# New tick tables for preparation and finishing, routing that ends one iteration later, rows of x that come one iteration earlier, and a fifth sum buffer

## The chip, the cores and the metric

One core of a Trainium2 chip runs the kernel. The metric is the device time of one launch in microseconds. TensorE (PE), VectorE (DVE), ScalarE (ACT), GpSimd (POOL) and SyncE (SP) each run their own instruction stream strictly in program order and meet only at semaphores. One profiled execution and three timed ones are at hand.

## The reference

For 16 batches of 128 rows of width 512, with 2048 context rows per batch:

```python
x = x + xattn(layernorm(x), ctx, ctx)   # 16 query heads of 32, ONE shared key head and value head
x = x + attn(layernorm(x))              # gated delta rule, 4 heads of 128, chunks of 64, needs inv(I - A0)
x = x + ffn(layernorm(x))               # top-1 routing to 16 experts, 128 rows each, relu(x w1) w2

# routing inside ffn
gate = softmax(xr @ Wg); idx = argmax(gate)
loc  = cumsum(onehot)[row, idx] - 1      # place of the row in its expert, over all earlier rows
valid = loc < C
dispatched[idx, min(loc, C)] = xr
```

All is float32. The count in `loc` runs over all 2048 rows, so the routing of one batch needs the counts of the batch before.

## The kernel before

The program has two blocks. `attention` handles the 16 batches; `experts` then runs the 16 experts from the rows that were scattered to DRAM. Only `attention` is touched.

`attention` is a software pipeline written by hand. The outer loop is `for i in range(-1, B + 1)`. Iteration `i` works on three batches at once: it does the softmax attention of batch `i`, prepares batch `i + 1` (norm of x, transposes of the context, keys, values, queries), and finishes batch `i - 1` (normalising the attention output, output projection, second norm, delta rule with six doubling levels, third norm, gate and routing). An iteration is cut into 128 ticks. Each engine's stream is generated by the same double loop over `i` and tick `t`, and a step is emitted at the tick that a table names. So the tables (`NORM`, `XN`, `XNT`, `QPROJ`, `TILE_AT`, `KV_AT`, `VT_AT`, `LOAD_AT`, `POST`, `LEVEL_AT`, `MAX_AT`) fix nothing but the order of each stream. A tick has no length of its own.

The steady work of batch `i`: at every even tick a score matmul (`score`, line 370) and its exponential on ACT (line 553). For each of four head groups 16 matmuls and DVE maxima of the next group (`largest`, lines 357 and 708), then the turn of the maxima (`turn_max`, line 362), whose row ACT copies (line 559) and SP sends. The probabilities times values in quads (`weigh`, line 382), two quads in one tick at ticks 1 and 17 of every group of 32. GpSimd adds up the probabilities over the 16 key blocks (`add_weights`, line 917) into one of four buffers `psum[g]`.

The seam between two batches matters for what follows. At tick 118 PE computes the gate logits (`lg`, line 508), DVE and ACT form the one-hot row (`oh`, lines 818 to 830), PE counts (`loc`, line 513, tick 123), DVE computes the target row in 14 small instructions (`row`, lines 834 to 860, tick 125), and GpSimd scatters. In the next iteration DVE normalises rows of x for the coming batch (lines 722 to 727, ticks 1 and 5), PE sums numerators and denominators (`sums`, line 396, tick 9), DVE takes four reciprocals (line 764, ticks 9 to 12) and multiplies (`att`, line 767, tick 13), and PE starts the output projection (`x1`, line 336 with `wo`, ticks 15 to 18). `sums` writes the same PSUM bank, `P_BANK`, that the routing read, and every later finishing step uses it too. The first addition into `psum[0]` of a batch waits for `sums` of the batch before (line 912). `TensorE` may issue the maxima matmul number n only when DVE has reduced number n - 2 (line 347).

Of the kernel before, what the change touches and what calls it, by code (L numbers as in the profile page):

```python
# [24 lines left out]
C_IDENT, C_UPPER, C_PAIR, C_ONES, C_DUMP, C_LEVEL = range(6)  # L25
# [24 lines left out]
PV_AT = [17, 17, 33, 33]  # L50
# [51 lines left out]
def attention(nc, T, w1_first, w1_in):  # L102
    with ExitStack() as ctx:
# [6 lines left out]
        def named(name, names):  # L110
# [30 lines left out]
        oS, psum = ([sb(f"{n}{g}", [P, 512]) for g in range(HG)] for n in ("oS", "psum"))  # L141
# [51 lines left out]
        post_pe = named("post_pe", "x1 xn2T V rkT I X1 Vn oT2 x2 xn3T lg loc")  # L193
        post_act = named("post_act", "ss0 ss1 ss2 ss3 xn2T rk0 rk1 rk2 rk3 V rkT X1 Vn oT2 xn3T eg")
        post_dve = named("post_dve", "x1 st2 mv2 xn2 XT1a MT IT x2 st3 mv3 xn3 lg0 lmax emax cand best oh "
                         "ohloc before loc valid locc row0 row d0 d1 sidx gate token token1")
        post_pool = named("post_pool", "xb ve2 rs2 x12 rm rn MT0 XT0 XT1 ve3 rs3")
# [3 lines left out]
        def level(b, lv, part=0):  # L201
# [5 lines left out]
        T_USES = [use for _, use in sorted(  # L207
            [(XNT, ("x", 0))] + [(t, ("t", k)) for k, t in enumerate(TILE_AT)]
            + [(t, ("v", c)) for c, t in enumerate(VT_AT)])]

        def turn_bank(b, use):
            return [T_BANK, *B_BANK, PV_BANK][T_USES.index(use) % 4] if b == 0 else T_BANK

        def turn_read(b, use):

            n = T_USES.index(use) - (4 if b == 0 else 1)
            if n < 0:
                return v_act.at(b - 1, 1) if b else None
            kind, i = T_USES[n]
            if kind == "x":  # L220
                return xnT_act.at(b)
            return cxT_act.at(b, i) if kind == "t" else v_act.at(b, i)
# [29 lines left out]
        def _(e):  # L252
# [30 lines left out]
            def send_queries(b):  # L283

                for part, src, ready in ((0, qh, q_act), (1, qh, q_act), (2, qs, q_pool)):
                    e.wait_ge(*ready.at(b))
                    for h in range(4):
                        e.dma_start(
                            qT[b % 2][part * HD:(part + 1) * HD, :].bitcast(F32).rearrange(
                                "d (g h t) -> d g h t", g=HG, h=4)[:, :, h, :],  # L290
                            src[h * HD:(h + 1) * HD, :].bitcast(F32).rearrange("d (g t) -> d g t", g=HG)).then_inc(
                            q_in.sem, 16)

            for i in range(-1, B + 1):
                for t in range(TICKS):
                    if t == XNT + 2 and i + 2 < B:
                        load_x(i + 2)
                    if t == QSEND and i + 1 < B:
                        send_queries(i + 1)
                    for b, g in groups_at(i, t, MAX_TURN):  # L300
                        send_max(b, g)
                    if t in LOAD_AT:
# [3 lines left out]
                    if t == 0 and i >= 1:  # L306
                        if i > 1:
                            e.wait_ge(*post_pe.at(i - 2, "Vn"))
# [3 lines left out]
                    if t == POST["store"] and i >= 1:  # L312
                        e.wait_ge(*post_dve.at(i - 1, "x2"))
                        e.dma_start(T["out"][i - 1], x2).then_inc(x2_out.sem, 16)
# [11 lines left out]
        def _(e):  # L326
# [59 lines left out]
            def sums(b):  # L386
# [3 lines left out]
                if b:  # L390
                    e.wait_ge(*post_dve.at(b - 1, "before"))
                if b + 1 < B:
                    e.wait_ge(*kvs_dve.at(b + 1, 3))
                for out, lhs, src in ((KV_BANK, cst[:, C_ONES, 0:HD], psum), (P_BANK, cst[:, C_STACK, 0:HD], oS)):
# [4 lines left out]
            def prepare(b, t):  # L399
# [6 lines left out]
                if t == QPROJ:  # L406
                    if b == 0:
                        e.wait_ge(*wq_in.at(0))
                    e.wait_ge(*kvs_dve.at(b, 0))
                    e.wait_ge(*xnT_act.at(b))  # L410
                if QPROJ <= t < QPROJ + HG:
                    cols = slice((t - QPROJ) * P, (t - QPROJ + 1) * P)
                    for c in range(DC):
                        ins = e.matmul(KV_BANK[:, cols], wq[:, c, cols], xnT[:, c, :], start=c == 0, stop=c == DC - 1)
                    if t == QPROJ + HG - 1:
# [10 lines left out]
                if t in KV_AT:  # L426
                    c = KV_AT.index(t)
                    e.wait_ge(*cxT_act.at(b, 4 * c + 3))
                    if c:
                        e.wait_ge(*kvs_dve.at(b, c - 1))  # L430
                    elif b:
                        e.wait_ge(*(o_dve.at(b - 2, "recip3") if b > 1 else kvs_dve.at(0, 3)))
                    if c == 1:
                        e.wait_ge(*q_dve.at(b))
# [10 lines left out]
            def finish(b, t):  # L445
# [3 lines left out]
                if t == POST["x1"]:  # L449
                    e.wait_ge(*o_dve.at(b, "att"))  # L450
                if POST["x1"] <= t < POST["x1"] + DC:
                    ins = project(P_BANK, turned, wo, t - POST["x1"])
                    if t == POST["x1"] + DC - 1:
# [4 lines left out]
                if t == POST["V"]:  # L458
                    e.wait_ge(*post_act.at(b, "xn2T"))
                if POST["V"] <= t < POST["V"] + DC:  # L460
                    ins = project(P_BANK, turned, ww, t - POST["V"])
                    if t == POST["V"] + DC - 1:
# [27 lines left out]
                if t == POST["Vn"]:  # L490
                    e.wait_ge(*xt_dve.at(*level(b, LEVELS - 1, 3)))
                    per_head(P_BANK, lambda h: cut(XT, h), lambda h: cut(V, h)).then_inc(post_pe.sem, 1)
                if t == POST["oT2"]:
                    e.wait_ge(*post_act.at(b, "Vn"))
                    per_head(P_BANK, lambda h: cut(Vn, h), lambda h: cut(IT, h)).then_inc(post_pe.sem, 1)
                if t == POST["x2"]:
                    e.wait_ge(*post_act.at(b, "oT2"))
                if POST["x2"] <= t < POST["x2"] + DC:
                    ins = project(P_BANK, turned, wr, t - POST["x2"])
                    if t == POST["x2"] + DC - 1:  # L500
                        ins.then_inc(post_pe.sem, 1)
                if t == POST["xn3T"]:
                    e.wait_ge(*post_dve.at(b, "xn3"))
                    transposes(P_BANK, lambda h: cut(xn3, h)).then_inc(post_pe.sem, 1)
                if t == POST["lg"]:
                    e.wait_ge(*post_act.at(b, "xn3T"))
# [3 lines left out]
                    ins.then_inc(post_pe.sem, 1)  # L510
                if t == POST["loc"]:
                    e.wait_ge(*post_dve.at(b, "oh"))
                    e.matmul(P_BANK[:, 0:E], cst[:, C_UPPER, :], oh[:], start=True, stop=False)
                    e.matmul(P_BANK[:, 0:E], cst[:, C_ONES, :], before[:], start=False, stop=True).then_inc(
                        post_pe.sem, 1)
# [710 lines left out]
```

## Time and profile before

| | us |
|---|---|
| median of 3 timed runs (2423.36 to 2426.57) | 2425.18 |
| profiled execution, its own time | 2427.98 |
| span in the profile | 2426.1 |

The span is the time from the first to the last instruction of the profiled execution. The rest of its own time, 1.9 us, lies around it. In the profile the main part of the program is the run of iterations 0 to 15, whose first exponentials start at 70.8, 162.9, 287.0 and from there about every 117.8 us up to 1817.7. The experts begin at 2001.5.

### The profile page before, as it was taken

The numbers are of one execution on the slowest core, as the hardware profiler recorded it, in microseconds if no ns is written. First come the engines' busy times: TensorE is split into PE (matmuls) and PEld (weight loads), VectorE is DVE, ScalarE is ACT, GpSimd is POOL, SyncE is SP. The second block draws the span as 40 slices with busy tenths as digits, with TensorE's granted clock in tenths as the row PEclk, the third lists the DMA queues.
The fourth block names the chain that finished last, engine by engine and source line by source line (L and its number), as shares of the span: only waits on it lengthen the run. The fifth ranks groups of instructions, "written<-read, shape, count | busy, mean of one in ns | idle before, by whom it ended". The sixth has DMA issues, their size and how long they took to land. (4 is left out here: it accounts for less than half of the span.)

```text
span 2426.1 us, 35019 instructions
## 1 busy us (share of the span) xinstructions
PE 2189.4 (90%) x12608; PEld 1429.9 (59%) x12608; DVE 1371.0 (57%) x2311; ACT 1193.3 (49%) x2237; POOL 1638.2 (68%) x1323
## 2 busy tenths in 40 slices
PE   5889898989998989898989898989898769999999
PEld 3435555546464646464646464645554448999998
DVE  2665757566667566666666666666665433333333
ACT  3555554646464646464645455555554313333333
POOL 0676878677777777777777777777777714655655
PEclk9889998999899989998999899989998889999999
DMA  4532120202020202121211111121120009999995
GB/s 160 188 113 66 40 82 24 83 23 83 23 83 23 83 26 80 40 66 40 66 47 58 51 59 63 43 66 42 59 79 9 18 14 375 350 363 346 362 363 189
DMA packets 108157, 263.75 MB, mean 109 GB/s; under 512 B 9849, under 2 KB 35065, under 8 KB 99792
## 3 DMA queue, kind: packets, MB, share of 16 engines
q1 hardware_dynamic: 98448, 235.32, 27.7%
q10 hardware_dynamic: 5952, 14.29, 1.6%
q0 software_dynamic: 3584, 11.90, 1.2%
q8 instruction: 101, 1.65, 0.3%
q14 instruction: 72, 0.59, 0.1%
HBM read 223.74 MB, written 25.72 MB: 103 GB/s over the span
## 5 line engine op out<-in xcount | busy, mean ns | idle before, releaser
L917 POOL TENSOR_TENSOR psum<-psum,p 128x512 f32<-128x512 f32 x896 | 1162.9, 1298 | 291.7 <-ACT p L553 197.7
L708 DVE TENSOR_REDUCE mpart<-bank 128x1 f32<-128x512 f32 x1024 | 675.0, 682 | 403.5 <-PE bank L357 396.1
L553 ACT ACTIVATE p<-bank 128x512 f32<-128x512 f32 x1024 | 596.8, 600 | 553.5 <-PE bank L370 543.6
L357 PE MATMUL bank<-kT,qT 96*128 96x512 f32 x1024 | 484.1, 480 | 62.6 <-DVE mpart L708 32.5
L370 PE MATMUL bank<-qT,kT 97*128 97x512 f32 x1024 | 502.4, 492 | 4.7 <-ACT p L553 4.0
L357 PEld LDWEIGHTS bank<-kT,qT 96*128 96x128 f32 x1024 | 199.6, 196 | 211.5 <-DVE mpart L708 104.6
L370 PEld LDWEIGHTS bank<-qT,kT 97*128 97x128 f32 x1024 | 201.7, 197 | 142.6 <-issue 113.6
L382 PE MATMUL bank<-p,v 128*32 128x512 f32 x2048 | 271.4, 651 | 0.0
L1159 POOL TENSOR_TENSOR w2l<-w,w2h 128x1024 fp32r<-128x1024 f32 x64 | 203.2, 3177 | 75.1 <-PE ebank L1074 54.4
L332 PE MATMUL bank<-cst,w_first 128*128 128x128 f32 x1024 | 164.1, 287 | 21.7 <-DMA w_first<-in_ctx 18.0
L332 PEld LDWEIGHTS bank<-cst,w_first 128*128 128x128 f32 x1024 | 134.3, 149 | 64.9 <-issue 29.4
L917 POOL TENSOR_TENSOR psum<-p 128x512 f32<-128x512 f32 x64 | 81.8, 1278 | 122.5 <-ACT p L553 101.6
L582 ACT COPY w_first<-bank 128x512 f32<-128x512 f32 x256 | 149.3, 586 | 15.0 <-PE bank L332 14.9
L1102 ACT ACTIVATE hh<-ebank 128x512 fp32r<-128x512 f32 x64 | 38.3, 599 | 225.3 <-PE ebank L1058 225.3
L1096 ACT CAST w2h<-w 128x2048 fp32r<-128x2048 f32 x64 | 121.5, 1898 | 44.1 <-DMA w<-in_w 44.1
L382 PEld LDWEIGHTS bank<-p,v 128*32 128x32 f32 x2048 | 56.7, 116 | 141.7 <-issue 107.3
L437 PE MATMUL bank<-w_first,wkv 128*64 128x512 f32 x512 | 125.7, 612 | 10.0 <-ACT w_first L582 9.8
L336 PE MATMUL bank<-wo,turned 128*128 128x512 f32 x128 | 90.3, 799 | 38.8 <-DVE turned L767 38.8
L1058 PE MATMUL ebank<-dT,w_first 128*128 128x128 f32 x1024 | 120.9, 279 | 0.9 <-DVE dT L1117 0.9
L1058 PEld LDWEIGHTS ebank<-dT,w_first 128*128 128x128 f32 x1024 | 120.0, 195 | 2.4 <-issue 1.2
L1123 DVE TENSOR_TENSOR w2l<-w,w2h 128x1024 fp32r<-128x1024 f32 x64 | 79.1, 1236 | 71.9 <-PE ebank L1074 48.0
L1128 DVE SCALAR_TENSOR_TENSOR hl<-ebank,hh 128x512 fp32r<-128x512 f32 x64 | 44.2, 691 | 133.4 <-ACT hh L1102 133.4
(159 smaller groups left out, 3137.8 us busy)
## 6 DMA issues: line engine op xcount, KB each, us to landing
w<-in_w SPq DMA_DIRECT2D x48, 2048.0 KB, 20.1
w_first<-in_ctx SPq DMA_DIRECT2D x64, 1024.0 KB, 4.9
w_first<-in_w SPq DMA_DIRECT2D x16, 2048.0 KB, 11.6
dispatched<-route ACTq DMA_DIRECT2D x17, 513.0 KB, 4.4
dis<-dispatched SPq DMA_DIRECT2D x16, 513.0 KB, 3.5
qT<-qh SPq DMA_DIRECT2D x128, 64.0 KB, 2.0
xin<-in_x SPq DMA_DIRECT2D x16, 256.0 KB, 2.6
qT<-qs SPq DMA_DIRECT2D x64, 64.0 KB, 2.0
```

What stands on the lines that cost most here:

```text
L332: ins = e.transpose(out[0:m, j * P:(j + 1) * P], src(j), ident)
L357: e.matmul(a[:], qT[b % 2][0:3 * HD, (4 * g + h) * P:(4 * g + h + 1) * P], kT[b % 2][0:3 * HD, c * 512:(c + 1) * 512], start=True, stop=Tr ...
L370: e.matmul(B_BANK[u % 2][:], kT[b % 2][0:3 * HD + 1, k * P:(k + 1) * P], qT[b % 2][0:3 * HD + 1, g * 512:(g + 1) * 512], start=True, stop= ...
L382: ins = e.matmul(PV_BANK[HD * j:HD * (j + 1), :], v1[b % 2][:, k + j, :], p[(UNITS * b + u + j) % NP][:], start=k == 0, stop=k == KB - 4)
L437: ins = e.matmul(KV_BANK[rows, :], wkv[:, j, :], cxT[c % 2][:, j, :], start=j < 2, stop=j >= 2)
L553: e.activation(p[n % NP][:], B_BANK[u % 2][:], ACT.Exp).then_inc(p_act.sem, 1)
L582: e.copy(cxT[c % 2][:, :, kk * P:(kk + 1) * P], turn_bank(b, ("t", k))[:].rearrange("p (c t) -> p c t", c=DC)).then_inc(cxT_act.sem, 1)
L708: e.tensor_reduce(mpart[g % 2][:, n:n + 1], A_BANK[(17 * g + n) % 2][:], AX.X, ALU.max).then_inc(max_dve.sem, 1)
L917: e.tensor_tensor(acc[:], first[:], p[(UNITS * b + u) % NP][:], ALU.add).then_inc(psum_pool.sem, 1)
L1058: ins = e.matmul(H_BANK[g][:, f * P:(f + 1) * P], w1[q][:, c, (4 * g + f) * P:(4 * g + f + 1) * P], dT[q][:, c, :], start=c == 0, stop=c = ...
L1096: e.copy(w2h[g][:], w2[q][:, 4 * g:4 * g + 4, :]).then_inc(w2h_act.sem, 1)
L1159: e.tensor_tensor(w2l[g % 2][:, 2:4, :], w2[q][:, 4 * g + 2:4 * g + 4, :], w2h[g][:, 2:4, :].bitcast(F32), ALU.subtract).then_inc(w2l_pool ...
```

## The change

The tables get new numbers. Rows of x are loaded, normalised and transposed an iteration earlier than the rest of a batch's preparation: `NORM`, `XN` and `XNT` become negative, that is ticks 81, 82 and 89 of the iteration before. The finishing of a batch now reaches past tick 127: `oh` is at 129, `loc` at 133, `row` at 135, which are ticks 1, 5 and 7 of the second next iteration. `sums` goes from tick 9 to 10, the reciprocals from 9 to 12 to 9, 12, 13, 14, `att` from 13 to 15, `x1` from 15 to 18 to 18 to 21. The context tiles, no longer four ticks apart, stand one to eight apart. All four loops run over `range(-2, B + 2)`, the last one only up to `TAIL`. The semaphores of finishing are split into an early and a late set. `KV_BANK` and the transpose banks get their waits from a computed order of uses. There are five buffers for the sums of probabilities instead of four, used in turn, and the wait for `sums` moves from the first group of a batch to the second. The constant `C_DUMP` moves into a free column of `C_STACK`. `send_queries` gets a wait for the last score matmul of two batches before. No arithmetic is changed.

```diff
-NORM, XN, XNT, QPROJ, QSEND = 1, 5, 10, 27, 38
-TILE_AT = [8 + 4 * k for k in range(KB)]
-KV_AT = [TILE_AT[4 * c + 3] + 3 for c in range(4)]
-VT_AT = [KV_AT[2 * m + 1] + 7 for m in range(2)]
-LOAD_AT = [t + 6 for t in TILE_AT[3::4]]
-POST = dict(xb=2, sums=9, recip=[9, 10, 11, 12], att=13, x1=15, x1_add=18, norm2=19, xn2=22, ss=23, x12=24, rn=24,
-            xn2T=25, rk=27, V=28, V_copy=31, rkT=34, I=38, XT1=40, X1=44, Vn=98, oT2=101, x2=104, x2_add=107,
-            store=108, norm3=108, xn3=111, xn3T=115, lg=118, eg=119, oh=120, loc=123, row=125)
-LEVEL_AT = [[47 + 9 * n, 50 + 9 * n, 53 + 9 * n] for n in range(LEVELS)]
-MAX_AT, MAX_TURN = [15 * n // 8 - 39 for n in range(KB)], -8
+NORM, XN, XNT, QPROJ, QSEND = -47, -46, -39, [22, 26, 27, 29], 32
+TILE_AT = [9, 13, 14, 16, 19, 23, 27, 32, 35, 40, 44, 51, 54, 58, 61, 69]
+KV_AT = [20, 36, 59, 74]
+VT_AT = [42, 79]
+LOAD_AT = [20, 46, 55, 71]
+POST = dict(xb=4, sums=10, recip=[9, 12, 13, 14], att=15, x1=[18, 19, 20, 21], x1_add=23, norm2=22, xn2=25, ss=29,
+            x12=32, rn=34, xn2T=34, rk=37, V=[37, 38, 39, 40], V_copy=40, rkT=42, I=45, XT1=44, X1=49, Vn=100,
+            oT2=102, x2=[106, 107, 108, 109], x2_add=110, store=116, norm3=114, xn3=119, xn3T=122, lg=127, eg=127,
+            oh=129, loc=133, row=135)
+LEVEL_AT = [[50, 53, 56], [59, 62, 65], [68, 71, 74], [77, 80, 83], [85, 88, 90], [94, 97, 102]]
+TAIL = POST["row"] + 1 - TICKS
+MAX_AT = [-40, -38, -36, -34, -32, -29, -28, -26, -24, -23, -21, -19, -17, -15, -13, -11]
+MAX_TURN, PV_AT = -9, [17, 17, 33, 33]
...
             def send_queries(b):
+                if b >= 2:
+                    e.wait_ge(*b_pe.at(b - 2, UNITS - 1))
...
-                acc = psum[g]
+                acc = psum[(HG * b + g) % 5]
                 if k == 1:
-                    if b and g == 0:
-                        e.wait_ge(*sums_pe.at(b - 1))
+                    if HG * b + g >= 5:
+                        e.wait_ge(*sums_pe.at((HG * b + g - 5) // HG))
...
-            for i in range(-1, B + 1):
-                for t in range(TICKS):
-                    if i + 1 < B:
+            for i in range(-2, B + 2):
+                for t in range(TICKS if i <= B else TAIL):
+                    if 0 <= i + 1 < B:
                         prepare(i + 1, t)
+                    if i + 2 < B:
+                        prepare(i + 2, t - TICKS)
...
-                    if i >= 1:
+                    if i >= 2:
+                        finish(i - 2, t + TICKS)
+                    if 1 <= i <= B:
                         finish(i - 1, t)
```

The first place is DVE's stream at the seam, from the end of the routing (the `token` instruction, line 860 of before and 902 of after, stands right ahead of both pieces) to the multiplication `att`. `mpart` is a maximum, `xin` is rows of x, `x` is the reciprocal buffer that shares a tile with `x1`, `turned` is the result of `att`. Before:

```order
L708 TENSOR_REDUCE mpart<-bank 128x1 x2
L722 BN_STATS st<-xin 128x6
L703 MEMSET pad_dve 128x1
L704 BN_AGGR mv<-st 128x2
L708 TENSOR_REDUCE mpart<-bank 128x1 x2
L727 TENSOR_SCALAR xin<-xin,mv,rs 128x512
L708 TENSOR_REDUCE mpart<-bank 128x1 x3
L764 RECIPROCAL x<-bank 128x128 x2
L708 TENSOR_REDUCE mpart<-bank 128x1
L764 RECIPROCAL x<-bank 128x128 x2
L708 TENSOR_REDUCE mpart<-bank 128x1
L767 TENSOR_TENSOR turned<-bank,x 128x512
```

The same stretch of DVE's stream in the changed kernel:

```order
L750 TENSOR_REDUCE mpart<-bank 128x1 x2
L806 RECIPROCAL x<-bank 128x128
L750 TENSOR_REDUCE mpart<-bank 128x1
L806 RECIPROCAL x<-bank 128x128
L750 TENSOR_REDUCE mpart<-bank 128x1
L806 RECIPROCAL x<-bank 128x128 x2
L750 TENSOR_REDUCE mpart<-bank 128x1
L809 TENSOR_TENSOR turned<-bank,x 128x512
```

The norm of the rows of x has left the stretch, and five maxima stand between the routing and `att` instead of nine.

The second place is PE's stream between `sums` and the first matmul of the output projection (`wo,turned`). `qT,kT` is a score, `kT,qT` a maximum, `cst,w_first` a context tile, `cst,xin` the rows of x, `p,v` a pair of quads of the weighted values. Before, from the instruction behind `sums`:

```order
L357 MATMUL bank<-kT,qT 128x512
L370 MATMUL bank<-qT,kT 128x512
L332 MATMUL bank<-cst,xin 128x128 x4
L357 MATMUL bank<-kT,qT 128x512
L370 MATMUL bank<-qT,kT 128x512
L332 MATMUL bank<-cst,w_first 128x128 x4
L357 MATMUL bank<-kT,qT 128x512
L370 MATMUL bank<-qT,kT 128x512
L357 MATMUL bank<-kT,qT 128x512
L336 MATMUL bank<-wo,turned 128x512
```

The changed kernel, where one more maximum stands between `sums` and the first row:

```order
L404 MATMUL bank<-qT,kT 128x512
L366 MATMUL bank<-cst,w_first 128x128 x4
L391 MATMUL bank<-kT,qT 128x512
L404 MATMUL bank<-qT,kT 128x512
L366 MATMUL bank<-cst,w_first 128x128 x4
L391 MATMUL bank<-kT,qT 128x512
L404 MATMUL bank<-qT,kT 128x512
L366 MATMUL bank<-cst,w_first 128x128 x4
L416 MATMUL bank<-p,v 32x512 x8
L391 MATMUL bank<-kT,qT 128x512
L404 MATMUL bank<-qT,kT 128x512
L370 MATMUL bank<-wo,turned 128x512
```

A pair of quads, a further tile and a further score now stand between `sums` and the projection, and the rows of x are gone.

## Rows read from the trace of the kernel before

**Rows 1.** Page: span, busy time, share and instructions by engine.

```profile
span 2426.1 us, 35019 instructions
PE 2189.4 (90%) x12608; PEld 1429.9 (59%) x12608; DVE 1371.0 (57%) x2311; ACT 1193.3 (49%) x2237; POOL 1638.2 (68%) x1323
```

**Rows 2.** Windows: stretch, length, busy PE, PEld, DVE, ACT, POOL; clock; DMA.

```profile
287.00:1817.70 1530.70, 1406.52 (x7905) 837.62 (x7904) 988.86 (x1695) 835.87 (x1690) 1141.41 (x990) 0.96 0.17 56
1923.30:2001.50 78.20, 47.74 (x224) 29.62 (x216) 26.71 (x92) 12.32 (x43) 13.62 (x20) 0.74 0.04 17
```

**Rows 3.** Windows inside iteration 8, 16 ticks each: ticks 0-15 and 32-47.

```profile
993.30:1011.50 18.20, 13.88 (x66) 5.92 (x65) 15.58 (x31) 6.66 (x13) 14.88 (x15) 0.88 0.13 45
1034.00:1048.00 14.00, 12.91 (x84) 8.42 (x84) 9.62 (x15) 9.68 (x20) 9.36 (x9) 1.00 0.44 131
```

**Rows 4.** Windows at the seam: gate logits to projection, then two stretches of low clock.

```profile
986.72:1009.06 22.34, 16.41 (x84) 8.07 (x83) 20.53 (x43) 10.15 (x21) 18.87 (x18) 0.92 0.15 48
1009.06:1012.70 3.64, 3.64 (x8) 2.11 (x9) 0.54 (x1) 0.99 (x2) 3.06 (x3) 0.53 0.01 2
992.20:995.60 3.40, 3.40 (x16) 1.15 (x18) 3.26 (x10) 1.28 (x3) 3.02 (x3) 0.50 0.01 5
```

**Rows 5.** Timeline of PE: start, length, instruction, [idle before it, and its releaser].

```profile
973.26 1.05 PE L340 MATMUL bank<-V,xr 128*128 128x128 f32 x8
975.00 1.16 PE L340 MATMUL bank<-rk,Y 128*128 128x128 f32 x8 [0.20 <-ACT Y L638]
...
990.81 0.40 PE L513 MATMUL bank<-oh,cst 128*128 128x16 f32 x2 [1.00 <-DVE oh L830]
991.28 0.48 PE L370 MATMUL bank<-qT,kT 97*128 97x512 f32 x1
991.60 0.39 PE L357 MATMUL bank<-kT,qT 96*128 96x512 f32 x1
...
1000.90 1.07 PE L396 MATMUL bank<-psum,cst 128*32 128x512 f32 x8
...
1009.06 1.93 PE L336 MATMUL bank<-wo,turned 128*128 128x512 f32 x2 [2.30 <-DVE turned L767]
...
1015.51 1.02 PE L336 MATMUL bank<-wo,turned 128*128 128x512 f32 x2
...
1062.23 1.92 PE L382 MATMUL bank<-p,v 128*32 128x512 f32 x16
```

**Rows 6.** Timeline of DVE: the same columns.

```profile
13.21 0.55 DVE L727 TENSOR_SCALAR xin<-xin,mv,rs 128x512 f32<-128x512 f32 x1 [1.03 <-POOL rs L922]
...
987.82 0.17 DVE L818 COPY lg<-bank 128x16 f32<-128x16 f32 x1 [0.30 <-PE bank L508]
...
988.67 0.17 DVE L823 TENSOR_REDUCE sc<-eg 128x1 f32<-128x16 f32 x1 [0.47 <-ACT eg L649]
...
992.63 0.17 DVE L834 TENSOR_TENSOR oh<-bank,oh 128x16 f32<-128x16 f32 x1
...
996.83 1.28 DVE L708 TENSOR_REDUCE mpart<-bank 128x1 f32<-128x512 f32 x2
998.02 0.68 DVE L722 BATCH_NORM_STATS2 st<-xin 128x6 f32<-128x512 f32 x1
...
1000.42 1.52 DVE L727 TENSOR_SCALAR xin<-xin,mv,rs 128x512 f32<-128x512 f32 x1 [0.32 <-POOL rs L922]
...
1003.89 1.76 DVE L764 RECIPROCAL x<-bank 128x128 f32<-128x128 f32 x2
```

**Rows 7.** Timeline of POOL: the same columns.

```profile
985.19 11.21 POOL L917 TENSOR_TENSOR psum<-psum,p 128x512 f32<-128x512 f32 x8
...
999.82 0.57 POOL L922 TENSOR_TENSOR rs<-rs,mhalf 128x1 f32<-128x1 f32 x1
```

**Rows 8.** Waits over the whole span: who for whom, us, times, longest.

```profile
POOL psum L917 <- PE bank L396: 21.0, 15, 1.9
PE bank L357 <- ACT mrow L559: 28.1, 31, 1.3
```

More of the change, by code:

```diff
@@ L24 @@
 ROUTE = 2 * D + 2
-C_IDENT, C_UPPER, C_PAIR, C_ONES, C_DUMP, C_LEVEL = range(6)
+C_IDENT, C_UPPER, C_PAIR, C_ONES, C_LEVEL = range(5)
 C_STACK = C_LEVEL + 6
@@ L140, in attention @@
         p = [sb(f"p{i}", [P, 512]) for i in range(NP)]
-        oS, psum = ([sb(f"{n}{g}", [P, 512]) for g in range(HG)] for n in ("oS", "psum"))
+        oS, psum = [sb(f"oS{g}", [P, 512]) for g in range(HG)], [sb(f"psum{g}", [P, 512]) for g in range(HG + 1)]
         mpart = [sb(f"mpart{i}", [P, 16]) for i in range(2)]
@@ L190, in attention @@
         o_dve = named("o_dve", "recip0 recip1 recip2 recip3 att")
[L193 to L197, printed above, removed]
+        post_pe = named("post_pe", "x1 xn2T V rkT I X1")
+        post_act = named("post_act", "ss0 ss1 ss2 ss3 xn2T rk0 rk1 rk2 rk3 V rkT X1")
+        post_dve = named("post_dve", "x1 st2 mv2 xn2 XT1a MT IT")
+        post_pool = named("post_pool", "xb ve2 rs2 x12 rm rn MT0 XT0 XT1")
+        late_pe = named("late_pe", "Vn oT2 x2 xn3T lg loc")
+        late_act = named("late_act", "Vn oT2 xn3T eg")
+        late_dve = named("late_dve", "x2 st3 mv3 xn3 lg0 lmax emax cand best oh ohloc before loc valid locc row0 row "
+                         "d0 d1 sidx gate token token1")
+        late_pool = named("late_pool", "ve3 rs3")
         y_pe, z_pe, xt_pe = count("y_pe", LEVELS), count("z_pe", LEVELS), count("xt_pe", LEVELS - 1)
@@ L311, in _ @@
                         e.dma_start(xr[:], T["x"][i - 1]).then_inc(xr_in.sem, 16)
-                    if t == POST["store"] and i >= 1:
-                        e.wait_ge(*post_dve.at(i - 1, "x2"))
-                        e.dma_start(T["out"][i - 1], x2).then_inc(x2_out.sem, 16)
+                    for b, at in ((i - 2, t + TICKS), (i - 1, t)):
+                        if at == POST["store"] and 0 <= b < B:
+                            e.wait_ge(*late_dve.at(b, "x2"))
+                            e.dma_start(T["out"][b], x2).then_inc(x2_out.sem, 16)
                     if t == LOAD_AT[3] and i == LAST - 1:
@@ L390, in sums @@
                 if b:
[L391 to L394, printed above, removed]
+                    e.wait_ge(*late_dve.at(b - 1, "before"))
+                e.wait_ge(*kv_read(b, ("s", 0)))
+                for out, lhs, src in ((KV_BANK, cst[:, C_ONES, 0:HD], [psum[(HG * b + g) % 5] for g in range(HG)]),
+                                      (P_BANK, cst[:, C_STACK, 0:HD], oS)):
                     for g in range(HG):
@@ L405, in prepare @@
                     transposes(turn_bank(b, ("x", 0)), lambda j: xin[:, j * P:(j + 1) * P]).then_inc(xnT_pe.sem, 1)
[L406 to L412, printed above, removed]
+                if t in QPROJ:
+                    m = QPROJ.index(t)
+                    if m == 0:
+                        if b == 0:
+                            e.wait_ge(*wq_in.at(0))
+                        read = kv_read(b, ("q", 0))
+                        if read is not None:
+                            e.wait_ge(*read)
+                        e.wait_ge(*xnT_act.at(b))
                     for c in range(DC):
-                        ins = e.matmul(KV_BANK[:, cols], wq[:, c, cols], xnT[:, c, :], start=c == 0, stop=c == DC - 1)
-                    if t == QPROJ + HG - 1:
+                        ins = e.matmul(KV_BANK[:, m * P:(m + 1) * P], wq[:, c, m * P:(m + 1) * P], xnT[:, c, :],
+                                       start=c == 0, stop=c == DC - 1)
+                    if m == 3:
                         ins.then_inc(q_pe.sem, 1)
@@ L428, in prepare @@
                     e.wait_ge(*cxT_act.at(b, 4 * c + 3))
[L429 to L434, printed above, removed]
+                    read = kv_read(b, ("k", c))
+                    if read is not None:
+                        e.wait_ge(*read)
                     for j in range(DC):
@@ L521, in _ @@
                     e.wait_ge(*dec_dve.at(DEC_DVE - 1))
-                for t in range(TICKS):
+                for t in range(TICKS if i <= B else TAIL):
                     if 0 <= i < B and t % 2 == 0:
                         score(i, t // 2)
-                    if i + 1 < B:
+                    if 0 <= i + 1 < B:
                         prepare(i + 1, t)
+                    if i + 2 < B:
+                        prepare(i + 2, t - TICKS)
                     for b, u in quads_in(i, t):
                         weigh(b, u)
-                    if i >= 1 and t == POST["sums"]:
+                    if 1 <= i <= B and t == POST["sums"]:
                         sums(i - 1)
@@ L965, in finish @@
                         in_=route[:], in_offset=None).then_inc(scat_out.sem, 16)
-            for i in range(-1, B + 1):
+            for i in range(-2, B + 2):
                 if i == 1:
```

266 lines of the change are left out of this document (148 added, 118 removed).

## Prediction

> **What bounds the kernel now.** I read the page first: PE is busy for 90% of the span, POOL 68%, DVE 57% [rows 1]. Then the windows. Thirteen steady iterations take 1530.7 us, 117.7 each, with PE busy for 1406.5, or 108.2 each; POOL is busy for 87.8 and DVE for 76.1 of it [rows 2]. So PE is the bound on average, and no other engine is close. But the slack is not spread evenly. Sixteen ticks in the middle of an iteration take 14.0 us with PE busy for 12.9; the first sixteen take 18.2 with PE busy for 13.9 and DVE busy for 15.6 [rows 3]. That stretch holds the seam between two batches. The window from the gate logits of one batch to the output projection of the next takes 22.34 us, with PE busy for 16.4 and DVE for 20.5 [rows 4]. The PE timeline names the two largest gaps in it: 1.00 us before the count, released by DVE's one-hot row, and 2.30 us before the projection, released by DVE's `att` [rows 5]. DVE has no gap longer than 0.47 us there [rows 6]. So at the seam DVE is the bound, and elsewhere PE. What shortens DVE's run at the seam, or puts more PE work beside it, is worth time; elsewhere only a removed PE gap is.
>
> **The seam, first the DVE run.** It goes from the copy of the logits at 987.82 to the end of `att`, where the projection starts at 1009.06: 21.2 us [rows 5, 6]. The change takes from it the statistics of x, 0.7, and the normalising of x, 1.5 [rows 6], and three of twelve maxima, 3 x 0.64 = 1.9, since two maxima take 1.28 [rows 6]. Counting them in the order: before, three ahead of the routing and nine behind; now four and five. That leaves 21.2 - 4.1 = 17.1. The wait of 0.47 for the exponential now has a maximum in it, which I leave uncounted. From the start of the logits' matmul to their copy is 1.1. So from logits to projection it is 18.2 us if DVE keeps its durations, against 22.3.
>
> **Then the PE work in it.** A score or a maximum matmul costs 0.32, start to start [rows 5]; a pair of quads 1.9, and `sums`, also 16 records of that shape, 1.9; four small matmuls of 128 columns 0.4 (eight take 1.05 with their tail); logits 0.9, count 0.5 [rows 5]. Before: 25 x 0.32 = 8.0, plus 0.9, 0.5, 1.9, 1.9 and three transposes 1.2, is 14.4. After: 20 x 0.32 = 6.4, plus 0.9, 0.5, two pairs 3.8, sums 1.9 and four tiles 1.6, is 15.1. The excess of the seam over its PE work is 22.3 - 14.4 = 7.9 before and 18.2 - 15.1 = 3.1 after. What is not in the seam is done elsewhere at PE's pace, so the iteration gains 4.8 us. Where it will stay late: DVE's routing, 4.2 us (992.63 to 996.83 [rows 6]), stands right before the maxima that PE needs at ticks 9 and 11, so I expect PE to wait there for some 2 us, behind `sums`, and again for under 1 us at the projection. Bounds: nothing but the 1.0 us gap before the count is saved, or all 7.9. This applies to the seams of iterations 2 to 15, 14 x 4.8 = 67 us.
>
> **The clock.** The steady stretch has a mean granted clock of 0.96 [rows 2], so 8% of it, 9.4 us per iteration, is at the lower level, 1.2 GHz. One stretch lies under the routing, where DVE decides (0.50 at 992.2), and costs nothing; one follows the 2.30 us gap, 0.53 from 1009.06 to 1012.7, where two projection records take 1.93 instead of 1.02 [rows 4, 5]. Half of 9.4 at half speed is 2.4 us per iteration. With gaps of about 2 us left I count on a third of it, 0.8 x 14 = 11 us; bounds 0 and 34.
> The Trainium skill's page TensorE: Matmul & The Clock Gate, section "What's actually happening", says that the slow clock is the default and that activity releases it. That agrees with the place of the second stretch, right behind the longest gap; by the rule alone, with no gap left at the seam, both stretches would go, and the sum would be 34 instead of 11.
>
> **The rest of the finishing.** Some distances shrink. From one small matmul group through an ACT copy to the next takes 1.74 us start to start, 0.9 of it behind the first group [rows 5]. Between `X1` and the first level now stands one score, 0.32: a gap of 0.6. Before `rkT` and `oT2` two ticks stand instead of three, 0.64 of work against 0.9: 0.3 each. The tiles at ticks 13, 14 and 16 share one bank and have to wait for its copy: 0.3 each for the two latter. Together 1.8 us per iteration. Others widen: the first maxima of a group wait for ACT's copy of the turned row, 28.1 us in all, 1.8 per iteration [rows 8]; that distance grows from two ticks to three, and half, 0.9, should go. The turn itself now stands two ticks behind its last maximum instead of three, which I leave within the bounds. Net +0.9 x 15 = +13 us; bounds -1.8 and +3 each, that is -27 and +45.
>
> **The early rows of x.** DVE normalises at tick 82 what POOL answers at 81. POOL may be within an addition, 11.21 / 8 = 1.4, and needs some 0.8 for the two small steps [rows 7], so DVE can stand still for 2.2 us. What is behind it are two maxima, the turn, and level 4. A pair of quads, 1.9, stands on PE at tick 81 and hides it: zero, bounds 0 and 2 per iteration. If POOL were several additions behind, this cover would be gone (a rival below). SP's load of x moves to tick 91, behind the transpose that it waits for, ahead of the store and a row of maxima at 119; both have room: zero.
>
> **Five buffers.** POOL's first addition waited for `sums`, 21.0 us in 15 times, 1.4 each [rows 8]. POOL is busy for 75% and 18 probability buffers lie between it and ACT, so nothing waits for it: zero. The waits of POOL at ticks 22 (for DVE's statistics one tick later) and 7 (for the routing, then the scatter) hold additions behind them, hidden by the same buffers. The wait in `send_queries` is for a score 34 ticks earlier; behind it stand the query DMAs and the next row of maxima: zero. `C_DUMP` is a change of address: zero.
>
> **The ends.** In the last iteration PE has no work beside the finishing, a chain of 78.2 us [rows 2]. The routing of batch 14, formerly hidden, now stands in front of its reciprocals: 4.2 us of routing and the one-hot row partly beside the last scores: +4, bounds 0 and 8. At the start x is transposed first instead of second: it was ready at 13.21 + 0.55 [rows 6], so zero, bounds 0 and 1.
>
> **The sum**, on the profiled execution's 2428.0 (span 2426.1 and 1.9 around it): -67 - 11 + 13 + 4 = -61, 2367. The median of the timed runs is 2.8 lower, so 2364; I say 2365.
>
> **Rivals.** *More than that.* In the routing the small DVE instructions take 4.2 us for 14 because POOL adds without a break beside them, 8 additions in 11.2 us [rows 7]; the same normalising takes 0.55 with POOL idle and 1.52 beside additions [rows 6]. Now POOL may have emptied its queue and be waiting for the routing itself. Then 14 x 0.15 = 2.1, 2.1 saved x 14 = 29, and with whole clock recovery 23 more: 2365 - 52 = 2313. For it: POOL's `sums` wait is gone, so it enters the seam with less backlog. Against: it is released by DVE only at the end.
> The Trainium skill's GPSIMD Engine Reference, section "Key points", says that GpSimd shares its SBUF interfaces with VectorE and contends with some DVE instructions. The two normalising rows agree; by that rule the moved normalising still costs 1.5, since additions run at tick 82 as well.
> *Nothing.* The seam gains but 4 us reappear, since the single-tick distances cost twice what I count and PE waits for the delayed maxima: 2425, within 0.2% (4.9 us, about what a measurement of this kernel can tell from no change). For it: every finishing step uses one bank and goes to another engine and back.
> *Slower.* POOL is behind when DVE asks it for the norm at tick 81. Each addition in its queue holds DVE for 1.4 us, and with it the maxima and the level. The cover is 1.9 and the gain 4.1 per iteration, so from five queued additions (7.0 us) the change loses; at seven, 9.8 + 0.8 - 1.9 - 4.1 = 4.6 too much by 15 is 2494, and at six 2473. For it: such queues of eight exist at the seam [rows 7]. Against: at tick 81 POOL has had 40 ticks without other work and is idle for a quarter of the time. A milder case, two late answers (22 and 81), gives 2440.
> *It doesn't do what it says* would be the same as nothing, and the order of the streams excludes it.
>
> **Chances and range.** Forecast 0.67 (own range 2335 to 2400, from half to one and a half of the sum), more 0.13, nothing 0.08, slower 0.12. Leaving out part of the best case and the slower one gives 2315 to 2418. Faster by over 0.2%: 0.79; within: 0.08; slower: 0.13.
>
> **What would show it.** In the new trace: logits to projection near 18 us with DVE busy throughout and no norm of x in it; no gap before the count; a gap of some 2 us on PE at the maximum behind `sums`, released by a DVE maximum; less than 1 us before the projection; steady iterations near 113.6 us; mean clock there above 0.96; gaps of half a microsecond before level 0 and at the tile of tick 14; at tick 82 a DVE wait for POOL of at most 2 us. I am wrong if the routing's maxima hold PE for 4 us or more, if iterations stay over 117, or if the tail grows by over 8.

## The result, and the profile after

The changed kernel takes 2260.7 us (median of 4, 2259.6 to 2264.4) against 2425.5. The ratio is 0.9323, 95% interval 0.9311 to 0.9335: 165 us less, well below the forecast of 2365 and outside its range. The page of the profiled execution, the lines that answer to [rows 1]:

```profile
span 2262.6 us, 35078 instructions
PE 2095.3 (93%) x12608; PEld 1404.6 (62%) x12608; DVE 1369.5 (61%) x2311; ACT 1187.9 (53%) x2237; POOL 1633.3 (72%) x1323
PEclk8789999999999999999999999999999779999999
```

All engines but PE are as busy as before. PE's own busy time fell by 94 us, though it runs the same 12608 matmuls: the first sign that the clock has a part in it. The windows, in the columns of [rows 2]: the thirteen steady iterations, one seam (logits to projection), the stretch from there to the next logits, and the chain at the end, up to the experts.

```profile
286.00:1665.40 1379.40, 1320.58 (x7904) 815.55 (x7900) 984.81 (x1687) 829.74 (x1691) 1136.68 (x987) 1.00 0.19 62
1134.11:1151.82 17.71, 14.90 (x98) 7.49 (x97) 17.06 (x36) 8.75 (x18) 16.36 (x15) 1.00 0.19 56
1151.82:1240.02 88.20, 86.45 (x513) 55.15 (x513) 58.82 (x96) 55.07 (x113) 71.17 (x63) 1.00 0.19 61
1757.40:1838.10 80.70, 52.52 (x235) 33.06 (x234) 29.91 (x104) 12.94 (x46) 15.34 (x21) 0.73 0.04 17
```

And the one stretch of before that [rows 4] did not hold, behind its seam:

```profile
1009.06:1103.89 94.83, 90.65 (x527) 55.85 (x527) 55.98 (x89) 54.17 (x110) 68.87 (x60) 0.98 0.17 56
```

A steady iteration went from 117.7 to 106.1 us. Of the 11.6 us, 4.5 went in the seam (22.3 to 17.8 as a mean of eleven iterations; DVE is busy for 20.5 and 17.1 us of the two seams shown) and 7.0 outside it (95.4 to 88.4). The stretch outside comes in two lengths before, 94.8 and 96.0 by turns, so the one shown is of the shorter kind.

Not all of the 7.0 is slack that went. The seam now holds 16 records of quads and 8 of context tiles more and five scores and maxima and the four transposes of x less, so by the prediction's prices 0.7 us of PE work moved from outside into the seam. That leaves 6.3. Time without any matmul fell from 4.2 to 1.8 us, and time at the lower clock level from 4.5 to 0.3; at half speed that is 2.1 us. For the remaining 1.8 us no view names a wait. I take them for waits so short that the modelled ends of matmuls cover them, which is not shown. PE's waits in one such stretch, before (1244.59 to 1339.45) and after (1151.82 to 1240.02); columns: who for whom, total us, times, longest (`turned` is the result of `att`, `mrow` the turned row of maxima, `xr` the delta rule's intermediate, `mneg` the reduced maxima that are about to be turned). Before:

```profile
PE bank L336 <- DVE turned L767: 2.3, 1, 2.3
PE bank L357 <- ACT mrow L559: 1.2, 1, 1.2
PE bank L488 <- DVE xr L802: 0.6, 2, 0.5
```

After:

```profile
PE bank L396 <- DVE mneg L757: 0.8, 1, 0.8
PE bank L374 <- ACT xn L667: 0.4, 1, 0.4
```

(The first row of before is the gap that ends at the projection, at the border of the window.) By phases, from the starts of the exponentials: first exponential 6.5 us later than before (77.3), iteration 0 longer by 7.0, iteration 1 shorter by 14.5, iterations 2 to 14 by 151.3, iteration 15 by 13.6, the end longer by 2.5 (78.2 to 80.7), the experts the same. Together 163.4; the spans differ by 163.5.

Inside the seam the forecast order is there. PE's timeline:

```profile
1139.13 0.39 PE L547 MATMUL bank<-oh,cst 128*128 128x16 f32 x2 [0.51 <-DVE oh L872]
...
1142.85 1.07 PE L430 MATMUL bank<-oS,cst 128*32 128x512 f32 x8
1145.59 0.50 PE L391 MATMUL bank<-kT,qT 96*128 96x512 f32 x1 [1.68 <-DVE mpart L750]
...
1151.82 1.11 PE L370 MATMUL bank<-wo,turned 128*128 128x512 f32 x2
```

DVE's, in the routing:

```profile
1141.04 0.69 DVE L877 TENSOR_TENSOR before<-before,oh 128x16 f32<-128x16 f32 x1
...
1142.15 0.80 DVE L886 TENSOR_TENSOR sc<-sc 128x1 f32<-128x1 f32 x1
1142.99 1.19 DVE L888 TENSOR_TENSOR sc<-sc,cst 128x1 f32<-128x1 f32 x1
...
1144.85 1.28 DVE L750 TENSOR_REDUCE mpart<-bank 128x1 f32<-128x512 f32 x2
```

The gap of 1.68 us is at the maximum behind `sums`, the projection waits for nothing, and the count waits 0.51 instead of 1.00. The routing takes 4.0 us. Three of its 14 instructions make that: the three shown with 0.69, 0.80 and 1.19.

### The profile page after: what moved, and what is told of

Read it like the earlier page. It is cut to its first block and busy times, and to the rows that moved or that the text cites. A ratio compares the mean times of both kernels' runs of the same rounds, so it can differ in the third digit from the quotient of the medians.

```text
span 2262.6 us, 35078 instructions
## 1 busy us (share of the span) xinstructions
PE 2095.3 (93%) x12608; PEld 1404.6 (62%) x12608; DVE 1369.5 (61%) x2311; ACT 1187.9 (53%) x2237; POOL 1633.3 (72%) x1323
## 5 line engine op out<-in xcount | busy, mean ns | idle before, releaser
L591 ACT ACTIVATE p<-bank 128x512 f32<-128x512 f32 x1024 | 590.3, 598 | 374.0 <-PE bank L404 365.5
L391 PE MATMUL bank<-kT,qT 96*128 96x512 f32 x1024 | 468.5, 464 | 34.6 <-DVE mpart L750 31.8
L404 PE MATMUL bank<-qT,kT 97*128 97x512 f32 x1024 | 484.1, 475 | 6.3 <-ACT p L591 4.8
L416 PE MATMUL bank<-p,v 128*32 128x512 f32 x2048 | 248.6, 603 | 0.0
L366 PE MATMUL bank<-cst,w_first 128*128 128x128 f32 x1024 | 158.5, 280 | 15.5 <-DMA w_first<-in_ctx 8.2
L366 PEld LDWEIGHTS bank<-cst,w_first 128*128 128x128 f32 x1024 | 126.1, 144 | 56.7 <-ACT w_first L620 19.8
L374 PEld LDWEIGHTS bank<-xn,x 128*128 128x128 f32 x768 | 94.3, 193 | 45.4 <-ACT xn L673 21.7
```

What stands on the lines that cost most here:

```text
L366: ins = e.transpose(out[0:m, j * P:(j + 1) * P], src(j), ident)
L391: e.matmul(a[:], qT[b % 2][0:3 * HD, (4 * g + h) * P:(4 * g + h + 1) * P], kT[b % 2][0:3 * HD, c * 512:(c + 1) * 512], start=True, stop=Tr ...
L404: e.matmul(B_BANK[u % 2][:], kT[b % 2][0:3 * HD + 1, k * P:(k + 1) * P], qT[b % 2][0:3 * HD + 1, g * 512:(g + 1) * 512], start=True, stop= ...
L416: ins = e.matmul(PV_BANK[HD * j:HD * (j + 1), :], v1[b % 2][:, k + j, :], p[(UNITS * b + u + j) % NP][:], start=k == 0, stop=k == KB - 4)
L591: e.activation(p[n % NP][:], B_BANK[u % 2][:], ACT.Exp).then_inc(p_act.sem, 1)
```

## The experiments

Each kernel but the fillers is the changed kernel with one edit; the fillers edit the kernel before. Times are medians in us; ratios are to the kernel before, run beside it, and "more" and "less" are against the changed kernel unless said otherwise. "Outside" is the stretch from the projection to the next logits.

**Rows of x back.** `NORM, XN, XNT = 1, 5, 10`.

> The changed kernel with the rows of x normalised and transposed at ticks 1, 5 and 10 again; all else new. If DVE's run at the seam decides (my theory), its 0.7 us of statistics and 1.5 us of normalising come back there: 14 x 2.2 = 31 us more, 2292, and up to 2325 if the slow clock returns with the longer gap (2.4 us per iteration). If the place of these two instructions does not matter and the tick distances did it all, 2261 within 5 us.

2303.0, ratio 0.9507 (0.9491 to 0.9523): 42 us more. Iteration 109.2, the seam 21.1 instead of 17.8, time at the lower clock 6.6 us per iteration instead of 0.5. In this order the loss is all in the seam: outside it the kernel takes 88.2, as before the edit. DVE's run at the seam decides.

**Four buffers.**

```diff
-                acc = psum[(HG * b + g) % 5]
+                acc = psum[g]
...
-                    if HG * b + g >= 5:
-                        e.wait_ge(*sums_pe.at((HG * b + g - 5) // HG))
+                    if b and g == 0:
+                        e.wait_ge(*sums_pe.at(b - 1))
```

> The changed kernel with four sum buffers and the old wait for the first group. Theory: POOL has slack, 2261 within 5 us. Rival (the fifth buffer frees POOL at the seam, so its additions are out of the way of DVE's small instructions): the 1.4 us of waiting per iteration come back and with them the contention, 20 to 45 us more, 2281 to 2306.

2256.4, ratio 0.9313 (0.9297 to 0.9328): no difference that the intervals separate, but inside much moved. POOL now stands still during the routing. POOL's and DVE's timelines and the seam's window:

```profile
1133.71 1.27 POOL L963 TENSOR_TENSOR psum<-p 128x512 f32<-128x512 f32 x1 [3.41 <-PE bank L430]
```

```profile
1131.51 0.16 DVE L886 TENSOR_TENSOR sc<-sc 128x1 f32<-128x1 f32 x1
1131.70 0.16 DVE L888 TENSOR_TENSOR sc<-sc,cst 128x1 f32<-128x1 f32 x1
```

```profile
1123.96:1139.71 15.75, 14.79 (x98) 7.58 (x98) 14.86 (x36) 8.76 (x18) 11.47 (x11) 1.00 0.13 36
```

The two instructions that took 0.80 and 1.19 take 0.16 each and the one with 0.69 takes 0.17; the routing falls from 4.0 to 1.8 us and the seam by 2.0, and 1.3 come back outside it. DVE's timeline there has a wait that the changed kernel does not have, in each of the thirteen iterations:

```profile
1151.22 1.51 DVE L818 TENSOR_SCALAR xn<-x,mv,rs 128x512 f32<-128x512 f32 x1 [1.25 <-POOL rs L968]
```

POOL has stood still for 3.4 us, is behind with its additions, and answers the second norm 1.25 us late. The fifth buffer is no part of the gain.

**POOL holds.** Five buffers, and POOL's first addition of a batch waits for the routing:

```diff
                 if k == 1:
+                    if g == 0 and b >= 2:
+                        e.wait_ge(*late_dve.at(b - 2, "token"))
```

> The changed kernel, five buffers, but POOL's first addition of a batch waits until DVE's routing of two batches before is done. The four-buffer run showed the routing at 1.8 us instead of 4.0 with POOL standing still. If it is POOL's additions beside the routing that stretch it (my theory): routing 1.8, seam near 15.7 us, 2250 to 2257, at or under the four-buffer kernel. If it was the absence of the fifth buffer by another way (POOL released by the sums only, so that reciprocals and transposes are undisturbed too): 2258 to 2261, routing 4.

2239.5, ratio 0.9232 (0.9213 to 0.9251): 21 us less than the changed kernel, and under the expected range. Timeline of POOL, then the seam and the steady iterations:

```profile
1124.59 1.27 POOL L965 TENSOR_TENSOR psum<-p 128x512 f32<-128x512 f32 x1 [2.27 <-ACT p L591]
```

```profile
1115.97:1131.74 15.77, 14.81 (x98) 7.59 (x98) 14.90 (x36) 8.78 (x18) 12.58 (x12) 1.00 0.14 37
282.10:1639.60 1357.50, 1320.80 (x7904) 813.00 (x7900) 961.77 (x1687) 829.97 (x1692) 1135.49 (x987) 1.00 0.19 63
```

POOL starts at 1124.59, when the routing has ended (the releaser shown is the one that the profile infers). The seam is as short as with four buffers, and outside it only 0.3 comes back (88.7 against 88.4): DVE does not wait for the second norm here, since POOL stood still for 2.3 us and not for 3.4. So it is the additions beside the routing that stretch it, and an added wait made the kernel faster. What is not solved by it: two small instructions ahead of the count (lines 867 and 872) still take 1.18 us each beside additions, against 0.24 and 0.23 in the last batch of the changed kernel, where POOL is idle.

**Hold, tuned.** On top of that, level 0 at 51, 54, 57 and `loc=134`.

> The kernel in which POOL waits for the routing, with level 0 a tick later (51, 54, 57) and the count at tick 134 instead of 133. PE waits 0.44 us ahead of level 0 and 0.50 ahead of the count. If a gap is worth its own length where the clock never falls: 14 x 0.9 = 13 us less, 2227. If the later steps make others late: 2235 to 2245.

2237.1, ratio 0.9226 (0.9210 to 0.9241), the best of all, though its interval overlaps the last one's. The two gaps went (0.94 us), 0.54 came up at a maximum at tick 6, and an iteration gained 0.3 us. Here a removed gap was largely taken by the next.

**Finishing of before.** The whole old table of finishing and levels, new preparation. (A level of the doubling is, on PE, a product Y, a product Z of what DVE made of Y, and transposes of what DVE subtracted Z from; its three ticks in `LEVEL_AT` are these.)

> The changed kernel with the whole table of finishing steps and levels of before (routing ends at tick 125 of the next iteration, output projection at tick 15), new tables of preparation, early rows of x. Theory (gaps at the seam and the slow clock behind them are the larger part of the 164 us): the rows stay early, so 2.2 of 4.5 us of the seam stay saved, the rest and most of the 2 x 2.4 us of slow clock come back, 2261 + 14 x 6 = 2345. Rival (the preparation tables carry the gain): at most 2290.

2503.0, ratio 1.0341 (1.0323 to 1.0358): 242 us more than the changed kernel, and slower than the kernel before. Theory and rival were both far off. The clock was at its lower level for 20 us of each iteration of 122.6, and PE waited some 2.2 us per iteration at the Z products of the levels, 2.0 at the longest.

**Rows of x alone.** All old tables, only the rows early (and the five buffers).

> All tick tables of before for finishing, tiles, keys, queries and maxima, but rows of x early (ticks 81, 82, 89), five buffers. If the seam's DVE run alone counts: 2.2 us per iteration less, 2425 - 31 = 2394. If the normalising at tick 82 stands in front of the Y step of level 4 (tick 83 in the old table) and holds PE there for 2 us, with slow clock behind it, as the run with the old finishing suggests: 2420 to 2440.

2451.1, ratio 1.0105 (1.0084 to 1.0126): 26 us slower than the kernel before, where moving the same rows back in the new order cost 42. DVE's timeline and PE's, at level 4:

```profile
1334.93 1.49 DVE L769 TENSOR_SCALAR xin<-xin,mv,rs 128x512 f32<-128x512 f32 x1 [0.44 <-POOL rs L968]
1336.94 0.67 DVE L836 TENSOR_TENSOR Y<-bank,cst 128x512 f32<-128x512 f32 x1
```

```profile
1337.67 1.16 PE L374 MATMUL bank<-xr,Y 128*128 128x128 f32 x8 [1.84 <-DVE Y L836]
```

The normalising at tick 82 stands ahead of DVE's step on Y of level 4, at tick 83 in the old table, and PE waits 1.84 us for it. The new table has that step at 85. POOL was not behind: its answer held DVE for 0.44. Nor did the seam gain what DVE no longer does there: it is 21.9 us, 0.4 less. DVE now stands idle in it and waits for PE's maxima, and the clock is at the lower level for 8.3 us of the seam:

```profile
1018.04 0.69 DVE L750 TENSOR_REDUCE mpart<-bank 128x1 f32<-128x512 f32 x1 [1.59 <-PE bank L391]
```

**Routing back.** The steps from `Vn` on at the old ticks.

> The changed kernel with only the late part of finishing, from Vn on, at the ticks of before, so that the routing ends inside the next iteration at tick 125. Theory: the DVE run from logits to projection grows by three maxima less the slack that it gains between routing and reciprocals, and the one-hot row gets its 1 us gap back: 10 to 30 us more, 2271 to 2291. Rival (the routing right ahead of the reciprocals is the bad part of the new order, since PE waits 1.7 us for the maximum behind the sums): faster than 2261 by up to 15 us.

2293.7, ratio 0.9466 (0.9450 to 0.9482): 33 us more. The gap before the count is 1.9 us and the clock is low for 5.3 us per iteration; the gap behind `sums` is gone. So the late routing is worth more than the gap of 1.7 us that comes with it.

**Projection early.** `x1=[16, 17, 18, 19]`, ahead of the pair of quads.

> The changed kernel with the output projection at ticks 16 to 19 instead of 18 to 21, in front of a pair of quads (1.9 us) that then no longer covers the wait for DVE. DVE's run stays as it is. If a gap costs its own length and the slow clock besides: gap 2 to 2.5 us, and a stretch at the lower clock behind it, 1.7 to 2.4 us: 14 x 4.3 = 60, 2321. If the gap costs only itself: 14 x 2 = 28, 2289. If the order merely shifts the wait (the quads are done later at no loss): 2261 to 2270, since PE's work behind the projection is the same.

2341.0, ratio 0.9658 (0.9641 to 0.9676): 80 us more, beyond even the case with the clock. In one iteration:

```profile
1193.27 2.07 PE L370 MATMUL bank<-wo,turned 128*128 128x512 f32 x2 [1.41 <-DVE turned L809]
1195.27 3.64 PE L416 MATMUL bank<-p,v 128*32 128x512 f32 x16
```

The pair of quads takes 3.64 instead of 1.92 [rows 5]. The seam keeps its 17.7 us, but with a pair of quads less in it. An iteration is 5.5 us longer. Time without any matmul grew by 2.7 of that, 1.8 of it in front of the projection and 0.8 at the queries; time at the lower clock rose by 4.7, at most 2.4 at half speed. The last 0.4 is open.

**Filler.** The kernel *before*, with PE work that nobody reads in the 2.3 us gap:

```diff
                 if t == POST["x1"]:
+                    if b + 2 < B:
+                        e.wait_ge(*cxT_act.at(b + 2, 1))
+                        for _ in range(2):
+                            e.matmul(T_BANK[:], ident, cst[:, C_LEVEL:C_LEVEL + 4, :], start=True, stop=True)
```

> The kernel before, with two 128x512 float32 matmuls whose result nobody reads (1.7 us of PE at full clock) put into the 2.3 us gap ahead of the output projection. They shorten no wait. If the slow clock behind the gap is caused by the gap and costs PE time: the clock stays high from the projection on, and 14 x 1.2 to 14 x 2.4 us go, 2391 to 2408. If the slow clock is a mere symptom or has another cause: 2425, or more where the filler is late (up to +10).

2394.0, ratio 0.9874 (0.9856 to 0.9891): 31 us faster by adding work. PE's timeline, then the windows of seam and rest:

```profile
1224.63 1.88 PE L453 MATMUL bank<-cst 128*128 128x512 f32 x4
1227.10 1.13 PE L336 MATMUL bank<-wo,turned 128*128 128x512 f32 x2 [0.59 <-DVE turned L771]
```

```profile
1204.77:1227.10 22.33, 18.26 (x88) 8.75 (x87) 20.51 (x43) 10.15 (x21) 18.85 (x18) 0.92 0.15 48
1227.10:1320.27 93.17, 89.00 (x526) 54.98 (x526) 56.01 (x89) 54.00 (x110) 68.86 (x60) 1.00 0.18 57
```

The seam stays 22.3, the projection starts at full clock (1.13 instead of 1.93 [rows 5]), and outside an iteration takes 93.2 instead of 95.4 as a mean, 2.2 us less. Time at the lower level went from 10.2 to 5.0 us per iteration, and outside the seam from 4.5 to nothing. So the gap causes the slow stretch behind it, and where PE decides such a stretch costs nearly half its length.

**Filler 2.** One more such matmul ahead of the count.

> The kernel before with the two filler matmuls of the filler run and one more, 0.9 us, in the 1.0 us gap ahead of the count. If the remaining slow stretch, under the routing, costs nothing since DVE decides there: 2394 within 5. If it costs half of its 5 us like the other: 2394 - 14 x 2.4 = 2360. The filler can also delay the count: up to +5.

2410.1, ratio 0.9930 (0.9907 to 0.9952): 16 us slower than with two. It made the seam 1.2 us longer and did not keep the clock up, so it does not say what the stretch under the routing costs.

**Preparation.** Five kernels put back parts of it:

```diff
 prep_old:     tiles every 4 ticks, KV_AT 23/39/55/71, VT_AT 46/78, QPROJ 27..30, QSEND 38, old LOAD_AT
 kvq_old:      the same with the new tiles and loads
 q_old:        QPROJ 27..30, QSEND 38
 kv_first_old: KV_AT[1] = 39, VT_AT[0] = 46
 kv_late_old:  KV_AT[2:] = 55, 71
```

> The changed kernel with the old ticks of context tiles, keys, values, query projection and loads; rows of x early, finishing new. Theory (seam and clock carry the gain, even spacing of tiles is as good): 2261 to 2275. Rival (the gain outside the seam, 7.0 us per iteration, comes from the places of the tiles and keys): 2261 + 15 x 5 = 2336.

> The changed kernel with the new ticks of context tiles but the old ones of keys, values and queries. The run with all of these old cost 88 us. If the even spacing of tiles is what cost it: 2261 to 2275. If the places of keys and queries among the levels are (each 1.9 us on PE, next to steps that wait for DVE): 2300 to 2350.

> The changed kernel with the query projection at ticks 27 to 30 (22, 26, 27, 29 in the new table) and its send at 38. If the queries carry the 88 us: 2300 or more. If the keys do: 2261 to 2272.

> The changed kernel with the second key and value matmul at tick 39 instead of 36 and the first value transpose at 46 instead of 42. The run with all old had 2.3 us more in ticks 32 to 47: 14 x 2.3 = 32, 2293. If the queries behind it were the reason: 2261 to 2270.

> The changed kernel with the third and fourth key and value matmul at ticks 55 and 71 instead of 59 and 74, that is 4 ticks behind its last tile at 51 and 2 behind the tile at 69, and next to the Z step of level 0 and between Y and Z of level 2. The run with all key and query ticks old had 3.3 us more in ticks 64 to 79 and 0.3 in 48 to 63: 14 x 3.6 = 50 us, 2311. If the gap hangs on the queries or on the value transposes instead: 2261 to 2275.

In this order: 2349.1 (ratio 0.9686, 0.9669 to 0.9704), 2349.5 (0.9689), 2286.2 (0.9431), 2284.6 (0.9417) and 2307.8 (0.9517, 0.9500 to 0.9535): 88, 89, 25, 24 and 47 us more. With the keys at their old ticks the tiles' places are worth nothing; keys, values and queries carry it, and the three parts add up to 96. Not all of it lies outside the seam: of the 6.6 us per iteration in prep_old 1.9 are in the seam and 4.7 outside, of the 6.0 in kvq_old 0.7 and 5.1. In kv_late_old at level 2:

```profile
1226.48 1.94 PE L471 MATMUL bank<-w_first,wkv 128*64 128x512 f32 x8 [0.20 <-ACT w_first L620]
1228.34 1.16 PE L374 MATMUL bank<-xr,Y 128*128 128x128 f32 x8
...
1231.80 0.50 PE L391 MATMUL bank<-kT,qT 96*128 96x512 f32 x1 [0.85 <-DVE mpart L750]
...
1233.46 1.16 PE L374 MATMUL bank<-xn,x 128*128 128x128 f32 x8 [0.56 <-ACT xn L673]
```

The same place in the changed kernel:

```profile
1201.04 1.16 PE L374 MATMUL bank<-xr,Y 128*128 128x128 f32 x8
...
1203.08 1.94 PE L471 MATMUL bank<-w_first,wkv 128*64 128x512 f32 x8
1204.94 0.66 PE L522 MATMUL bank<-cst,xr 128*128 128x128 f32 x4
...
1206.30 1.16 PE L374 MATMUL bank<-xn,x 128*128 128x128 f32 x8
```

The 1.9 us of keys stand behind the Z product, where they cover DVE's subtraction that the transposes (line 522) wait for. Ahead of Z they cover nothing, and two gaps of 0.85 and 0.56 appear behind. For keys 3 and 4 the cover is so shown; for the first value transpose and the queries it is argued from the times alone. In q_old the wait for the turned row of maxima is back, once per iteration:

```profile
1064.89 0.50 PE L391 MATMUL bank<-kT,qT 96*128 96x512 f32 x1 [1.33 <-ACT mrow L597]
```

**Maxima of before.** The old `MAX_AT` and `MAX_TURN = -8`.

> The changed kernel with the old ticks of maxima and of their turn (two ticks between turn and next group's second maximum instead of three). If the wait for ACT's copy of the turned row, 1.8 us per iteration before, was what went outside the seam: 15 x 0.9 to 15 x 1.8, 2275 to 2288. Rival (PE's order around it hides the wait): 2261 within 5.

2273.7, ratio 0.9378 (0.9361 to 0.9395): 13 us more. That is just under what was expected if the wait for the turned row came back, but it did not come back: the steady iterations of this run have none, where the kernel before has 1.85 us per iteration. Of the 0.9 us that an iteration is longer 0.6 lies in the seam.

## Why the prediction was wrong

The direction held, and so did the seam's working. It predicted 18.2 us from logits to projection and 17.8 was measured; its 4.8 us per iteration, work moved into the seam included, were 5.2; a 2 us gap behind `sums` was 1.7; the gap before the count, promised gone, halved. The end was to cost 4 and cost 2.5. In the changed kernel DVE's normalising at tick 82 cost PE nothing that shows; that this hangs on the new place of level 4 the prediction did not see (rows alone: 1.84 us).

The step that failed is "What is not in the seam is done elsewhere at PE's pace", and with it the +13 us for "the rest of the finishing". It took everything outside the seam as PE work, while 6.3 of those 95.4 us were slack. It listed the steps of finishing whose distance shrank, and has no term at all for the new places of keys, values and queries. Their worth is as cover: the runs that put them back cost 88 us, 4.7 to 5.1 us per iteration of it outside the seam. The listed items were off too, in the same direction: the shrunk distances were to cost 1.8 us per iteration and show as 0.9 (0.44 at level 0 and 0.45 at the tiles, nothing at `rkT` and `oT2`), and of the wait for the turned row half of 1.8 was to go and all of it went. Only the turn, left within the bounds, was dearer: PE waits 0.8 us there, which it did not before. With bounds of -27 and +45 the term could not hold what was there.

The second mis-sized term is the clock: 0.8 us per iteration, at most 2.4. Lower-level time fell from 10.2 to 0.5 us per iteration. The filler run prices one of the two stretches at 2.2; with the other the bound by half speed is 4.8. That the stretch under the routing "costs nothing" was not shown by any run, and the share that was lost under waits stays open. The rule of the Trainium skill's TensorE: Matmul & The Clock Gate, section "What's actually happening", would have given 34 us for it; the traces side with it (clock 0.96 before, 1.00 after), although gaps of up to 1.7 us are left.

The rival "more than that" had the right side and the wrong reason. POOL does not leave the routing alone in the changed kernel: it still takes 4.0 us. That it would take about 2.1 undisturbed was right, 1.8, but it needed an added wait. The kernel before shows the 1.8 as well: in the last batch, with POOL idle, its routing takes 1.83 us instead of 3.4 to 4.3, and the same two instructions read:

```profile
1994.74 0.16 DVE L844 TENSOR_TENSOR sc<-sc 128x1 f32<-128x1 f32 x1
1994.94 0.16 DVE L846 TENSOR_TENSOR sc<-sc,cst 128x1 f32<-128x1 f32 x1
```

"Five buffers: zero" held only as a net of 2.0 lost at the seam and 1.3 won outside. The Trainium skill's GPSIMD Engine Reference, section "Key points", names this contention, for VectorE instructions with two SBUF inputs among others, and the rows agree: 0.16 against 0.80 and 1.19.

The seam and the rest, as measured, give 13 x 11.6 = 151 us, and the other iterations and the ends the 12 missing to 163.5. What was not shown is what the 1.8 us per iteration without a named wait are, and why the start is 6.5 us later (three traces of kernels with the old start lie between 70.0 and 73.0, so some of it is scatter).

## What to carry to other kernels

In a pipeline ordered by hand, ask of every large independent piece of work on the bounding engine which wait it covers, and move it there: behind the step whose answer is late, not ahead of it. Edits of such tables do not add up: early rows of x gain 42 us in the new order and lose 26 in the old, so test a part in the order that it belongs to. A gap on TensorE costs up to its own length and, where it brings the low clock and PE decides behind it, nearly half of the slow stretch that follows. And look at what runs beside a chain of tiny VectorE instructions: holding GpSimd back for 2.3 us per iteration bought 21 us, while holding it for 3.4 us gave 1.3 of the 2.0 us per iteration back, since it then answered late elsewhere.

## What was unexpected of the hardware

Adding 1.9 us of useless matmuls per iteration saved 2.2 us per iteration. Some small VectorE instructions took 0.16 us with GpSimd idle and up to 1.19, about one GpSimd addition of 1.27, beside its additions. It hit those with two tiles as inputs (lines 877, 886 and 888) and the two on 128x16 ahead of the count (lines 867 and 872); one-input steps on 128x1 took 0.13 to 0.17 in both cases. Nor did the reciprocals of 128x128 that read PSUM: two took 1.75 us beside additions, and four took 3.39 with GpSimd idle.
